# Between two expert layers: two batches' rows taken from SBUF by one-hot products, their gates gathered behind the sixth scatter

## The reference

```python
def _L0_ffn_ref(x, router_w, w1, b1, w2, b2):
    ...
    top_w, top_idx = jax.lax.top_k(probs, K)
    top_w = top_w / (jnp.sum(top_w, axis=-1, keepdims=True) + 1e-09)
    ...
    sel = jnp.take_along_axis(y, top_idx[:, :, None], axis=1)
    out = jnp.einsum('tkc,tk->tc', sel, top_w)
    return out.reshape(Bb, Nn, Cc)
...
x = x + _L0_ffn_ref(_L0_cond_ref(x, ...), ...)
x = x + _L1_ffn_ref(_L1_cond_ref(x, ...), ...)
```

## Time and profile before

| | us |
|---|---|
| median of 3 runs | 163.36 |
| lowest, highest | 161.14, 163.69 |
| span of the profiled execution, first to last instruction | 150.0 |
| TensorE busy | 138.6 (92%) |
| VectorE busy | 94.5 (63%) |
| ScalarE busy | 84.9 (57%) |
| GpSimd busy | 61.4 (41%) |

### The profile page before, as it was taken

One profiled execution on the slowest core, in us unless ns is written; L12 is line 12 of the kernel. 1 busy time (PEld: TensorE's weight loads), 2 busy tenths in 40 slices (PEclk: granted clock), 3 DMA queues, 4 the chain that ended last, 5 costly groups with the idle time before them and its releaser, 6 DMA issues.

```text
span 150.0 us, 3681 instructions
## 1 busy us (share of the span) xinstructions
PE 138.6 (92%) x1139; PEld 122.1 (81%) x1139; DVE 94.5 (63%) x323; ACT 84.9 (57%) x259; POOL 61.4 (41%) x65
## 2 busy tenths in 40 slices
PE   7999887999999999999999997979998999999970
PEld 3765777999999999964789975748988999999960
DVE  5467947555556565452699777767242597748891
ACT  0688826777777666620377769985326255557400
POOL 5000376544477555560500000003677778777000
PEclk9999999999999999999999999999999999999996
DMA  4999614999999991113602940030022222457714
GB/s 142 357 403 315 216 37 89 312 367 393 394 396 342 300 331 37 38 36 88 211 0 116 400 190 0 0 153 2 19 56 50 56 50 59 152 174 236 254 47 140
DMA packets 12965, 26.10 MB, mean 174 GB/s; under 512 B 2082, under 2 KB 5538, under 8 KB 12562
## 3 DMA queue, kind: packets, MB, share of 16 engines
q1 hardware_dynamic: 10336, 21.54, 40.9%
q0 software_dynamic: 1760, 3.67, 8.1%
q10 hardware_dynamic: 850, 0.66, 1.3%
HBM read 19.92 MB, written 5.93 MB: 172 GB/s over the span
## 4 chain that ended last, share of the span: by engine, by line
PE 68%; DVE 14%; DMA 5%; issue 4%; ACT 3%; POOL 3%; DVEq 0%; ACTq 0%
PE bank L617 13%; PE bank L627 13%; PE bank L709 10%; PE bank L818 7%; PE bank L676 3%; PE bank L581 3%; DVE c_tok L1416 2%; POOL xg L476 2%; PE bank L685 2%; DMA got<-picked 2%; PE bank L508 2%; PE bank L770 2%; DMA xg<-rows,idx 2%; DMA picked<-y,sidx 1%; PE bank L543 1%
## 5 line engine op out<-in xcount | busy, mean ns | idle before, releaser
L952 ACT ACTIVATE hT<-bank,w_now 128x128 f32<-128x128 f32 x88 | 25.1, 368 | 11.5 <-PE bank L617 11.5
L1032 ACT ACTIVATE h1T<-bank,c_sb 128x256 f32<-128x256 f32 x44 | 18.3, 471 | 13.7 <-PE bank L709 13.7
L454 POOL DMA_INDIRECT xs<-rows,gidx x15 | 15.1, 1006 | 24.1 <-DVE gidx L1186 14.6
L627 PE MATMUL bank<-w_sb,hT 128*128 (+1 forms) x184 | 24.4, 276 | 0.3 <-ACT hT L952 0.3
L617 PE MATMUL bank<-xg,w_now 128*128 (+1 forms) x176 | 23.4, 276 | 0.8 <-ACT xg L936 0.8
L627 PEld LDWEIGHTS bank<-w_sb,hT 128*128 128x128 f32 x184 | 22.4, 192 | 0.5 <-ACT hT L952 0.5
L617 PEld LDWEIGHTS bank<-xg,w_now 128*128 128x128 f32 x176 | 21.4, 192 | 1.1 <-issue 1.0
L459 POOL DMA_INDIRECT picked<-y,sidx x16 | 15.7, 979 | 10.0 <-DVE y L1233 8.5
L476 POOL DMA_INDIRECT xg<-rows,idx x14 | 14.8, 1054 | 5.0 <-issue 3.7
L1233 DVE SCALAR_TENSOR_TENSOR y<-bank,pairm,y 128x128 f32 (+1 forms) x23 | 8.1, 351 | 10.2 <-PE bank L627 10.0
L709 PE MATMUL bank<-xgT,v_sb 128*128 128x256 f32 x56 | 14.2, 384 | 0.0
(11 more groups left out here) (214 smaller groups left out, 246.9 us busy)
## 6 DMA issues: line engine op xcount, KB each, us to landing
v_sb<-in_v SPq DMA_DIRECT2D x16, 256.0 KB
cw_sb<-in_cond_w SPq DMA_DIRECT2D x8, 386.5 KB
plane<-y SPq DMA_DIRECT2D x5, 512.0 KB, 5.1
w_sb<-plane SPq DMA_DIRECT2D x10, 256.0 KB, 3.1
w_sb<-in_w SPq DMA_DIRECT2D x2, 1024.0 KB, 7.6
w_sb<-in_w SPq DMA_DIRECT2D x1, 1290.0 KB, 7.9
w_sb<-in_w SPq DMA_DIRECT2D x1, 774.0 KB, 5.8
rows<-row SPq DMA_DIRECT2D x1, 544.0 KB, 3.3
```

Source lines behind the costliest of these rows:

```text
L454: pool.indirect_dma_start(out=xs[:, b % RING], out_offset=None, in_=rows0, in_offset=rows_at(gidx, b)).then_inc(gathered[b % RING], 16)
L627: mm = pe.matmul(bank[6 + j % 2][:, 0:C], hT[:, j % 2, P * f:P * f + P], w2_sb[:, bass.ds(e * (NF * C) + f * C, C)], start=(f == 0), stop= ...
L952: ins = act.activation(hT[:, j % 2, P * f:P * f + P], bank[2 + j % 2][:, P * f:P * f + P], ACT.Relu, bias=w1_of[:, F + f:F + f + 1])
L1032: act.activation(h1T[:, n % 2, fc], bank[UP_BANKS[(2 * n + h) % 4]][:, CAP * f:CAP * f + CAP], ACT.Gelu, bias=c1_sb[:, e * NF + fc:e * NF ...
```

## The change

In words:

- `picked` is doubled. The rows of batches 0 and 1 (`EARLY` = 2) that lie in the last three sorted blocks (`LATE` = 3) are scattered to the second half, where nobody reads them. Their places in the first half are cleared beforehand from a zeroed tile (`no_rows`) by two DMAs of SyncE, near the start.
- So batches 0 and 1 are read as soon as 13 scatters have landed, by two DMAs of SyncE (`early_in`). What the last three blocks hold for them is added on TensorE, straight from `y0` in SBUF: `late_rows` multiplies a block's rows by a one-hot matrix times the gate, `late_1h`. Three blocks and two batches make six matmuls.
- `late_1h` needs the gate of each sorted row. So `wt` is computed within the steps j = 1 to 3 of VectorE's loop, written to `gates` in DRAM by SyncE, and gathered by GpSimd in three gathers of 128 single values, behind the sixth scatter (`GATES_BEHIND` = 6). The indices, diagonals and one-hot matrices are made in VectorE's loop, between `bias` and `keep`.
- The other six batches are read in two pieces, when all 16 scatters have landed; ScalarE issues its two reads behind `silu(0)`.
- TensorE, ScalarE and VectorE take batches 0 and 1 through the batch stage first, down to `turn_d(1)`, and then run the pipeline over batches 2 to 7. x1 in rows of batches 0 and 1 is turned back by TensorE (`turn_back`) and copied by ScalarE. The 24 filler matmuls are gone.

The diff, cut to its core:

```diff
-        picked = nc.dram_tensor("picked", (K * T, C), F32).ap()
+        picked = nc.dram_tensor("picked", (2 * K * T, C), F32).ap()
+        gates = nc.dram_tensor("gates", (K * T, 1), F32).ap()
...
-        PIECES = [(0, 1), (1, 2), (2, 4), (4, NC)]
+        PIECES = [(EARLY, 4), (4, NC)]
...
+            sp.wait_ge(y0_cleared, 2)
+            for k in range(K):
+                load(picked_of(k, 0, EARLY), no_rows, picked_cleared)
...
+                if e == 2:
+                    sp.wait_ge(wt_ready, 1)
+                    load(gates.rearrange("(k p c) o -> p k (c o)", k=K, p=P), wt[:], gates_written)
...
-            sp.wait_ge(scattered, NB * 16)
+            sp.wait_ge(scattered, FIRST_LATE * 16)
+            for k in range(K):
+                load(got[:, k, 0:EARLY], picked_of(k, 0, EARLY), early_in)
+            sp.wait_ge(scattered_late, LATE * 16)
...
+                if b < FIRST_LATE:
+                    pool.indirect_dma_start(out=picked, out_offset=rows_at(sidx, b), in_=y0[:, b],
+                                            in_offset=None).then_inc(scattered, 16)
+                else:
+                    pool.indirect_dma_start(out=picked, out_offset=rows_at(late_idx, b - FIRST_LATE), in_=y0[:, b],
+                                            in_offset=None).then_inc(scattered_late, 16)
+
+            def gather_gate(i):
+                pool.wait_ge(gates_written, 16)
+                pool.indirect_dma_start(out=late_gate[:, i:i + 1], out_offset=None, in_=gates,
+                                        in_offset=rows_at(sidx, FIRST_LATE + i)).then_inc(late_gates_in, 16)
...
             for b in range(NB):
+                if b == GATES_BEHIND:
+                    for i in range(LATE):
+                        gather_gate(i)
                 scatter(b)
...
+            def late_rows(b, i):
+                pe.wait_ge(y_kept, min(FIRST_LATE + i + E, NPAIR))
+                return pe.matmul(bank[b][:, 0:P], y0[:, FIRST_LATE + i], late_1h[:, i, P * b:P * b + P],
+                                 start=False, stop=(i == LATE - 1))
+
             pe.wait_ge(in_x, 16)
-            for b in range(TURNED_SUMS):
+            pe.wait_ge(late_1h_ready, 1)
+            for b in range(EARLY):
                 pe.matmul(bank[b][:, 0:P], x_sb[:, b], ident, start=True, stop=False)
-            keep_warm(bank[4], 24)
+                for i in range(LATE - 1):
+                    late_rows(b, i)
             pe.wait_ge(in_cw, 16 * NC)
 
+            def sum_early(b):
+                pe.wait_ge(gate_diag_ready, 1)
+                pe.wait_ge(early_in, 32)
+                for k in range(K):
+                    pe.matmul(bank[b][:, 0:P], got[:, k, b], gate_diag[:, b, k], start=False, stop=False)
+                late_rows(b, LATE - 1).then_inc(x1_turned, 1)
+
+            def turn_back():
+                for b in range(EARLY):
+                    mm = pe.transpose(bank[6][:, P * b:P * b + P], x1T[:, b], ident)
+                mm.then_inc(x1_back, 1)
...
+            sum_early(0)
+            sum_early(1)
+            up_gate(0)
+            up_gate(1)
+            turn_back()
+            down1(0)
+            down1(1)
+            turn_d(0)
+            turn_d(1)
+            for b in range(EARLY, NC + 3):
+                if b < NC:
                     turn_x1(b)
...
+            take_x1(0)
+            take_x1(1)
+            silu(0)
+            act.wait_ge(scattered_late, LATE * 16)
+            for h, (c0, c1_) in enumerate(PIECES):
+                act.dma_start(got[:, 1, c0:c1_], picked_of(1, c0, c1_)).then_inc(got_in[h], 16)
+            silu(1)
+            act.wait_ge(x1_back, 1)
+            act.activation(x1[:, 0:EARLY].rearrange("p c d -> p (c d)"), bank[6][:, 0:EARLY * P], ACT.Copy).then_inc(x1_copied, 1)
+            take_d(0)
+            take_d(1)
+            squash(0)
+            take_row(0)
+            squash(1)
+            take_row(1)
...
+                if j == NPAIR - 4:
+                    v.wait_ge(late_gates_in, 16 * LATE)
+                    v.wait_ge(y0_cleared, 3)
+                if NPAIR - 4 <= j < NPAIR - 4 + LATE:
+                    i = j - (NPAIR - 4)
+                    ins = v.tensor_scalar(late_1h[:, i], token_key[:], late_token[:, i:i + 1], late_gate[:, i:i + 1],
+                                          ALU.is_equal, ALU.mult)
...
+            gate_up(0)
+            gate_up(1)
+            for c in (2, 3):
+                add_first(c)
+                add_second(c)
+            for b in range(EARLY, NC):
+                for c in {2: (4, 5), 3: (6,), 4: (7,)}.get(b, ()):
                     add_first(c)
                     add_second(c)
                 gate_up(b)
-                if b >= 2:
-                    score_batch(b - 2)
+                score_batch(b - 2)
```

More of the change, by code:

```diff
@@ L715, in _ @@
             pe.wait_ge(in_v, 16 * 2 * E)
-            for b in range(NC + 3):
-                if b < NC and b != TURNED_SUMS:
+            sum_early(0)
[9 more added lines that the diff above has]
+                if b < NC:
                     turn_x1(b)
-                if 0 <= b - 1 < NC:
+                if EARLY <= b - 1 < NC:
                     up_gate(b - 1)
-                if b == TURNED_SUMS:
-                    turn_x1(b)
                 if b > NC:
                     up1(0, 0, (b - NC - 1,))
-                if 0 <= b - 3 < NC:
+                if EARLY <= b - 3:
                     turn_d(b - 3)
-                if 0 <= b - 2 < NC:
+                if EARLY <= b - 2 < NC:
                     down1(b - 2)
@@ L963, in _ @@
                 take_h(j - 1)
-            act.wait_ge(scattered, NB * 16)
-            for h, (c0, c1_) in enumerate(PIECES):
-                act.dma_start(got[:, 1, c0:c1_], picked_of(1, c0, c1_)).then_inc(got_in[h], 16)
             def take_x1(b):
@@ L1234, in keep, with gates_and_late @@
                                        ALU.add).then_inc(y_kept, 1)
+            def gates_and_late(j):
+                if j == 1:
+                    v.wait_ge(exp_ready, 2)
+                    link(v.tensor_reduce(zsum[:], expd[:], AX.X, ALU.add))
+                    link(v.scalar_tensor_tensor(den2[:], zsum[:], 1e-9, den[:], ALU.mult, ALU.add))
+                if j == 2:
+                    link(v.tensor_scalar(den2[:], den2[:], 1.0, None, ALU.add))
+                    link(v.reciprocal(wt[:, 0], den2[:]))
+                if j == 3:
+                    v.tensor_tensor(wt[:, 1], wt[:, 0], den[:], ALU.mult).then_inc(wt_ready, 1)
+                    v.wait_ge(wt_ready, 1)
+                if j == 4:
+                    late = sidx[:, FIRST_LATE:NB]
+                    v.tensor_copy(late_token[:], gidx[:, FIRST_LATE:NB])
+                    link(v.tensor_scalar(late_batch[:], late, NC - 1, None, ALU.bitwise_and))
+                    link(v.tensor_scalar(late_shift[:], late_batch[:], float(EARLY), float(K * T), ALU.is_lt, ALU.mult))
+                if j == 5:
+                    v.tensor_tensor(late_idx[:], sidx[:, FIRST_LATE:NB], late_shift[:], ALU.add).then_inc(late_idx_ready, 1)
+                if j in (6, 7):
+                    for k in range(K):
+                        ins = v.tensor_scalar(gate_diag[:, j - 6, k], ident_sb[:], wt[:, k, j - 6:j - 5], None, ALU.mult)
+                    if j == 7:
+                        ins.then_inc(gate_diag_ready, 1)
+                if j == NPAIR - 4:
[5 more added lines that the diff above has]
+                                          ALU.is_equal, ALU.mult)
+                    if i == LATE - 1:
+                        ins.then_inc(late_1h_ready, 1)
             v.wait_ge(in_b2, 16)
@@ L1295, in _ @@
             v.wait_ge(in_cw, 16 * NC)
-            add_first(0)
-            add_second(0)
-            add_first(1)
-            add_second(1)
-            for b in range(NC):
-                for c in {0: (2,), 1: (3,), 2: (4, 5), 3: (6, 7)}.get(b, ()):
+            gate_up(0)
[5 more added lines that the diff above has]
+                for c in {2: (4, 5), 3: (6,), 4: (7,)}.get(b, ()):
                     add_first(c)
```

72 lines of the change are left out of this document (39 added, 33 removed).

## The result

The changed kernel took 167.21 us (median of 6 runs), the kernel before 162.75 beside it: ratio 1.018 [1.011, 1.025], slower by 1.8%. The forecast was 162.0 in a range up to 164.6, so it was wrong in sign and in size.

The account below looks back on a forecast made before the run. Latencies from the last `keep` to the picked rows, then TensorE in the batch stage, were taken as the bound. Gains 0.95 + 0.45 = 1.4 us; 150.0 - 1.4 = 148.6, with 13.4 around it 162.0 us, range 160.2 to 164.6.

Parts of the forecast that it names:

- with 13.4 us around it: Last step of the sum: 13.4 us outside the profile's span, added to 148.6 to give 162.0 us.
- Part 3: Three gates' gathers behind the sixth scatter on GpSimd's queue: cost 0.2 us at scatter 13, nothing at the 16th.
- Part 1 and 2: Clearing, doubled `picked`, gate write, small GpSimd operations at the start, and VectorE's new loop operations: cost nothing.
- Part 4: Early reads after scatter 13 lands at 64.1: in at 67.2, bounds 66.4 to 68.5.
- The estimate of 66.8: Early reads' arrival by the skill's DMA fit, before TensorE is ready; the gain would be 0.2 larger.
- Rival A: Early reads late, at 68.5: gain only 0.1, 163.3 us; chance 0.16.
- Parts 5 to 7: New order in the batch stage: `up_gate(2)` at 75.1 gains 0.95, from there to `up_gate(7)` 0.45, together 1.4 us.
- Part 8: The 24 filler matmuls go: no cost as long as TensorE's clock stays up.
- rival C: TensorE's clock falls in thin work from 70.4 to 75.1: 165.6 us, or 167.4 with three batches; chance 0.12.
- Rival D: Gates' gathers hold GpSimd at 1.83 + 0.30 each, scatter 13 is 2.7 late: 164.6 us; chance 0.08.
- Handing on the gain "in full": Behind the batch stage nothing changes and every score is needed, so the gain at 90.83 passes on in full.

Follow-up runs that it names:

- o1: The changed kernel, unchanged, run again on the short level: ratio 0.999 [0.993, 1.004] to the kernel before.
- f2: The changed kernel, unchanged, run again on the long level: 167.38 us, ratio 1.019 to the kernel before.
- f3: The changed kernel without the gates' write and three gathers, late gates constant 0.5, long level: 162.63 us, ratio 0.994 to the kernel before.
- m2: The kernel before plus three unused gathers of 128 single values behind the sixth scatter, long level: ratio 1.024 to the kernel before.
- k3: The kernel before with three GpSimd memsets of 0.95 us each behind the sixth scatter, short level: ratio 1.000 [0.996, 1.003].
- k1: The changed kernel with gates spread by four TensorE products, no gates' write or gathers, short level: 151.19 us, ratio 0.991 to the kernel before.
- f1: The kernel before, unchanged, run again on the long level: 164.54 us, ratio 1.007 against itself.
- m1: The changed kernel, unchanged, run again on the long level: ratio 1.016 [1.003, 1.029] to the kernel before.
- m3: The changed kernel with gates spread by four TensorE products, no gates' write or gathers, long level: 160.96 us, ratio 0.982 to the kernel before.
- n2: The kernel before with every scatter held back two steps (the last can't be), long level: ratio 0.997 [0.991, 1.002].
- g2: The changed kernel with one gates' gather each behind scatters 6, 8 and 10: ratio 1.018 [1.011, 1.025] to the kernel before.

## Why the prediction was wrong

**The sum against 163.36.** The step "with 13.4 us around it" failed. The measured rest is 1.8 us (170.19 - 168.4 in after, 152.02 - 150.2 in o1). The gap should have told me that the profile and the timed runs were not of one kind. This term did not set the sign. 148.6 + 1.8 = 150.4, a ratio of 0.991, was in fact my forecast for the short level; o1 gave 152.02 in the profiled run, 152.67 in the median, and 0.999.

**Part 3, the gates' gathers.** This carries the sign. It priced them on GpSimd's queue alone: 1.28 apiece, "cost 0.2 there". That queue behaved as priced: spacing 1.26 to 1.30, and on the short level 6th to 13th scatter 12.83 us against my 12.80. What it left out is that on the long level a dense row of indirect DMAs comes with late signals from TensorE to the other engines; my term for the gathers was 0.2 us there and nothing at the 16th scatter. On that level A is 16.7 to 17.7 where I had 12.8: 3.9 to 4.9 us, of which C keeps 2.0 to 4.4, the gain of the later parts taken off already (74.3 to 76.7 against 72.3), and the medians differ by 4.75 (f2 - f3). The Trainium skill (DMA: Bandwidth & Descriptors, Rules for kernel authors) says to coalesce many small transfers, since "under 64 KB you're paying mostly overhead"; each gather here moves 512 bytes. It speaks of the transfer's own time, which nobody waited for; what the other engines paid is in m2's rows.

**Part 1 and 2, nothing.** Held: with the new operations of VectorE and the clearing in place, but no gathers, A is 12.6 (f3). The first gather starts 0.8 later in o1 than in the profile of before (18.26 against 17.46), but k3, which has no clearing, shows 18.06, so I put nothing down to it.

**Part 4.** On the long level the reads are issued 2.26 us after scatter 13 (forecast 2.24) and are in by 78.24, 3.55 after the issue (taken 3.1, bounds 2.3 and 4.4). TensorE waited 0.17, since its own products were ready later as well (5.7 after scatter 13, where I had 5.2): that the reads' extra 0.45 cost nothing is luck. The estimate of 66.8, 2.7 after their issue, was 0.85 too low. In o1 the reads are in by 68.08, 3.1 after the issue, and nothing waits. Rival A did not come.

**Parts 5 to 7, the gain.** Right in mechanism and near in size. `up_gate(2)` starts 8.0 us after the 16th scatter in o1 and 8.1 in after, forecast 8.4, before 9.35. From there to the last `up_gate` pass it took 8.73 in both, forecast 8.65 to 8.7, before 9.13. B is 16.8 to 17.3 in the changed kernel, 18.2 to 18.6 in before: a gain of 0.9 to 1.8, forecast 1.4. What holds `up_gate(2)` in after is the turn of batch 2 behind `turn_d(1)`, as said, but only just. The rows of batch 2 come 3.0 us after ScalarE's issue at 80.79 (3.25 in o1), where I took 2.3, and in o1 the turn waits for them (VectorE's first add in after, the turn in o1):

```profile
83.80 0.35 DVE L1364 SCALAR_TENSOR_TENSOR bsc<-got,wt,x_sb 128x128 f32<-128x128 f32 x1 [0.85 <-DMA got<-picked]
```

```profile
74.66 0.14 PEld L724 LDWEIGHTS bank<-ident_sb,c_tok 128*128 128x128 f32 x1 [0.18 <-DVE c_tok L1368]
```

**Part 8 and rival C.** The clock stayed at 1.00 where I doubted it, so C did not come at its place. It fell in the first layer and near 144, at stretches in which TensorE stood for 2.66 and 3.12 us. By the Trainium skill (TensorE: Matmul & The Clock Gate, HAM oscillation) waits for data between short bursts bring the clock down. The trace agrees at these full stops; the window at 81.64, with waits under 1 us and 2.88 us of work in 3.96, shows 1.00.

**Rival D** named the right instructions and the right sign, with the wrong mechanism: a gather takes 0.97 us, not 1.83, and the scatters are not late for GpSimd's sake. Its time, 164.6, was still 2.6 below what was measured.

**Handing on the gain "in full"** did not show on the short level. C is 1.9 us shorter in o1 than in before, and the stretch behind it 1.2 longer (60.34 against 59.13). k3, which is before there, has 60.02, so most of that is what one profile differs from the next. The medians still show o1 at 0.999 and k1 at 0.991.

**What stays open.** What delays TensorE's signals, and what puts a program on one level or the other. Whether GpSimd's being busy or the DMAs set it off on the long level. Where the other 2.1 of the 4.75 us between the medians of f2 and f3 lie. Why the changed kernel's 1.9 us at C leave nothing in the median of the short level, when k1 keeps its own.

## What to carry to other kernels

Compare the profile's span with the timed runs before pricing anything: here 1.8 us belong outside the span, so a gap of 13.4 meant that the profile was of another level than the timed runs. Price an indirect DMA not on its queue alone: on the long level three in a row 1.3 us apart cost 2 to 4 us here, where the engines hand work to each other every microsecond. If a small table must change partitions in such a stretch, four products on TensorE did it here for 0.9 us of its time and turned a loss of 1.8% into a gain of 1.8% on that level; on the short one neither version lost time.

## What the runs showed that I had not expected

- The same program takes 152.6 or 163.6 us, on the same chip at different times. The long level has a stall of 2.4 to 2.7 us behind the first three scatters (f1, after, f2, f3, m1 to m3), the short level has none (before, k1, k3, o1), with the same spacing of 1.3; m3 has the stall at 1.30 and 1.29.
- In such a stall ScalarE, VectorE and SyncE resume together (48.81, 48.97, 48.93 in after), though each waits for another instruction of TensorE. ScalarE's signal to TensorE is in time meanwhile (0.14 us at 50.09 and at 61.03).
- With the first scatters 1.5 us apart or more the stall did not come (n2, one profile); one gather between two scatters was enough to bring it (g2, a stall of 1.6 us).
- A stop of 2.66 us costs more than itself: the granted clock is 0.62 in the mean from 50.09 to 54.40, with TensorE busy all the time.
